# A residual graph-network kernel on one core: first pair's hop 2 in whole float32, bias sum ahead of it, square weights by partition, nine warm-up products, and another order of the last roots and stores

## The reference

```
Xw = x @ Wv + bv;  sj = Xw @ aw[:d];  si = Xw @ aw[d:]
alpha = adj * exp(leaky_relu(sj + si + ab, 0.2))
T = alpha / (rowsum(alpha) + 1e-12)
H = sum over k=0..2 of (T^k x) @ Wk[k] + bk[k]
x = layernorm(x + relu(H))
x = layernorm(x + (adj @ x) @ w)
```

## Time and profile before

| | us |
|---|---|
| median of 3 runs | 272.7 (272.46 to 272.84) |
| profiled execution, whole time | 272.39 |
| its span, first to last instruction | 270.6 |
| PE busy in the span | 264.1 |
| DVE busy | 216.7 |
| ACT busy | 193.0 |
| POOL busy | 191.5 |

### The profile page before, as it was taken

The page is one execution under the profiler, slowest core; times in us unless marked ns, Lnnn a source line. Parts: engine busy times, 40 slices in busy tenths (PEclk is TensorE's granted clock), DMA queues, the critical chain, the costliest instruction groups (busy, mean ns, idle before and its releaser), DMA issues.

```text
span 270.6 us, 6025 instructions
## 1 busy us (share of the span) xinstructions
PE 264.1 (98%) x1890; PEld 246.1 (91%) x1890; DVE 216.7 (80%) x615; ACT 193.0 (71%) x439; POOL 191.5 (71%) x412
## 2 busy tenths in 40 slices
PE   8899999999999999999999999999999999999992
PEld 5899999999999999999999999999999999999991
DVE  0777798888889888888988888988888898788984
ACT  4887767777666777766777766677776667766874
POOL 4665567778877778887777887777788777657533
PEclk9999999999999999999999999999999999999999
DMA  7997486828955488446873484943884457932214
GB/s 242 274 185 94 85 48 218 131 72 147 168 137 159 81 133 117 155 143 156 140 117 80 154 155 137 152 153 51 131 160 100 118 116 75 125 99 78 80 41 155
DMA packets 28342, 34.91 MB, mean 129 GB/s; under 512 B 6803, under 2 KB 16150, under 8 KB 28310
## 3 DMA queue, kind: packets, MB, share of 16 engines
q1 hardware_dynamic: 27888, 34.12, 60.8%
q10 hardware_dynamic: 422, 0.40, 0.4%
HBM read 26.09 MB, written 8.42 MB: 128 GB/s over the span
## 4 chain that ended last, share of the span: by engine, by line
PE 95%; DMA 2%; DVE 1%; SPq 0%; ACT 0%; issue 0%
PE ps_v L1107 31%; PE ps_y L1107 17%; PE ps_out L1107 15%; PE ps_h L1107 11%; PE ps_agg L1271 10%; PE ps_v L1204 3%; PE ps_v L1208 3%; PE ps_v L1206 3%; DMA WY_sb<-Wk_dram 2%; PE ps_agg L1107 2%; DVE last_out_sb L884 0%; PE ps_v L1254 0%; PE ps_h L1245 0%; PE ps_y L1245 0%; PE ps_agg L1254 0%; DVE WY_lo L669 0%
## 5 line engine op out<-in xcount | busy, mean ns | idle before, releaser
L1107 PE MATMUL ps_v<-WX_hi,XT_hi 128*128 128x512 f32 (+1 forms) x132 | 49.0, 371 | 0.0
L1107 PE MATMUL ps_v<-WX_lo,XT_hi 128*128 128x512 f32 (+1 forms) x132 | 48.6, 368 | 0.0
L1107 PE MATMUL ps_v<-WX_hi,XT_lo 128*128 128x512 f32 (+1 forms) x132 | 48.6, 368 | 0.0
L1029 POOL TENSOR_TENSOR XT_lo<-xt,XT_hi 128x512 fp32r<-128x512 f32 x32 | 42.1, 1319 | 6.6 <-ACT XT_hi L426 6.6
L1039 POOL TENSOR_TENSOR alpha<-exps,adjs 128x256 f32<-128x256 f32 x31 | 23.1, 744 | 28.9 <-ACT exps L470 28.8
L1043 POOL TENSOR_TENSOR alpha_lo<-alpha,alpha_hi 128x256 fp32r<-128x256 f32 x31 | 22.8, 735 | 19.4 <-ACT alpha_hi L479 19.4
L1107 PE MATMUL ps_y<-WY_hi,XT_hi 128*128 128x258 f32 x116 | 35.2, 303 | 0.6 <-DVE WY_lo L673 0.6
L503 ACT ACTIVATE y<-res,offset,rstd 128x256 f32<-128x256 f32 x62 | 33.6, 591 | 2.2 <-POOL offset L1005 2.2
L1271 PEld LDWEIGHTS ps_agg<-adjs,y 128*128 128x128 f32 x248 | 32.0, 191 | 2.2
L1271 PE MATMUL ps_agg<-adjs,y 128*128 128x128 f32 x248 | 32.7, 275 | 0.0
L1107 PE MATMUL ps_y<-WY_lo,XT_hi 128*128 128x258 f32 x116 | 32.7, 282 | 0.0
(11 more groups left out here) (179 smaller groups left out, 830.8 us busy)
## 6 DMA issues: line engine op xcount, KB each, us to landing
xt<-xt_dram SPq DMA_DIRECT2D x32, 256.0 KB, 5.7
nodes<-nodes_dram SPq DMA_DIRECT2D x32, 256.0 KB, 5.8
out_dram<-out_sb SPq DMA_DIRECT2D x30, 256.0 KB, 5.3
adjs<-adjs_dram SPq DMA_DIRECT2D x32, 128.0 KB, 5.7
spread<-si_rows_dram SPq DMA_DIRECT2D x29, 128.0 KB, 4.7
si_rows_dram<-scores SPq DMA_DIRECT2D x29, 1.0 KB, 3.9
WvT_sb<-WvT_dram SPq DMA_DIRECT2D x1, 260.0 KB, 3.6
W_sb<-Wk_dram ACTq DMA_DIRECT2D x1, 256.0 KB, 3.3
```

The source lines that it names most:

```text
L1029: pool.tensor_tensor(XT_lo[k % 7][:].rearrange("p c b i -> p (c b i)"), xt_sb[k % 4][:], XT_hi[k % 7][:].rearrange("p c b i -> p (c b i)") ...
L1107: last = pe.matmul(to, a, b, start=start and n == 0, stop=stop and n == 2, skip_group_check=True)
```

## The change

WY_sb gets two more columns, into which DVE copies the score weights, so that pair 0's hop 2 multiplies whole float32 operands (`first_hop2`) and needs neither WY_hi nor WY_lo. WY_lo is then made in one subtraction, behind W1's low part. Pair 1's hop 2 (`second_hop2`) does its six hi-by-x products first and those with XT_lo after them. `sum_of_biases` stands ahead of `score_shift` and writes to ps_v; bk_hi_of is ACT's first step, and bias_of_hops one of DVE's first. Half of hop2_and_scores(2) goes ahead of propagate_v2(0). load_xt(4) waits for y_done. W0, W1, W2 and w are laid out by partition on the host, 2 KB in one piece each (W2 with two zero columns in each chunk). keep_warm runs nine products. In the tail ACT takes root 0 between the two halves of pair 29's normalisation, DVE splits `last_normalise2` into inverse and output with the inverse of graph 0 ahead of the moments of graph 1, and SP stores graph 0 of pair 31 before the half of pair 30.

```diff
--- before.py
+++ after.py
@@ -16,11 +16,11 @@
 
-def resnorm_graph_kernel(nc, xt, adjs, nodes, WvT, Wk, bk, w, si_rows, out):
+def resnorm_graph_kernel(nc, xt, adjs, nodes, WvT, W0, W1, W2, bk, w, si_rows, out):
     PAIRS = nodes.shape[0]
-    D = w.shape[0]
+    D = bk.shape[1]
     C = D // P
-    HOPS = Wk.shape[0]
+    HOPS = bk.shape[0]
@@ -42,7 +42,7 @@
         W1_sb = sb("W1_sb", [P, C, D])
-        WY_sb = sb("WY_sb", [P, C, D])
+        WY_sb = sb("WY_sb", [P, C, D + 2])
@@ -122,7 +122,7 @@
         ps_shift = ps_agg[:, 1, 0:1]
-        ps_bias = ps_y[:, 0, 0:D]
+        ps_bias = ps_v[:, 1, 0:D]
@@ -309,6 +309,7 @@
 
+        first_X = xt_sb[0][:].rearrange("p (c b i) -> p c b i", c=C, b=PER)
@@ -319,7 +320,7 @@
 
-                    sp.wait_ge(h_done, 1)
+                    sp.wait_ge(y_done, 1)
@@ -359,8 +360,8 @@
             def load_Wk(n):
-                to = (W0_sb, W1_sb, WY_sb)[n]
-                sp.dma_start(to[:], Wk[n].rearrange("(c p) n -> p c n", p=P)).then_inc(Wk_loaded[n], DMA)
+                to, held = ((W1_sb, W1), (WY_sb, W2))[n - 1]
+                sp.dma_start(to[:].rearrange("p c n -> p (c n)"), held).then_inc(Wk_loaded[n], DMA)
@@ -397,18 +398,21 @@
                     load_adjs(4)
-                    sp.dma_start(w_sb[:], w.rearrange("(c p) n -> p c n", p=P)).then_inc(w_loaded, DMA)
+                    sp.dma_start(w_sb[:].rearrange("p c n -> p (c n)"), w).then_inc(w_loaded, DMA)
...
 
+            def store_last(b):
+                sp.wait_ge(last_out_ready, b + 1)
+                sp.dma_start(out[LAST, :, b * D:(b + 1) * D], last_out_sb[:, b]).then_inc(last_stored, DMA)
+
+            store_last(0)
...
             sp.dma_start(out[LAST - 1, :, 0:D], out_sb[(LAST - 1) % 3][:, 0]).then_inc(last_stored, DMA)
-            for b in range(PER):
-                sp.wait_ge(last_out_ready, b + 1)
-                sp.dma_start(out[LAST, :, b * D:(b + 1) * D], last_out_sb[:, b]).then_inc(last_stored, DMA)
+            store_last(1)
@@ -416,7 +420,7 @@
         def _(act):
-            act.dma_start(W0_sb[:], Wk[0].rearrange("(c p) n -> p c n", p=P)).then_inc(Wk_loaded[0], DMA)
+            act.dma_start(W0_sb[:].rearrange("p c n -> p (c n)"), W0).then_inc(Wk_loaded[0], DMA)
@@ -436,7 +440,7 @@
                 act.wait_ge(Wk_loaded[2], DMA)
-                act.activation(WY_hi[:, :, 0:D], WY_sb[:], ACT.Copy).then_inc(WY_hi_ready, 1)
+                act.activation(WY_hi[:, :, 0:D], WY_sb[:, :, 0:D], ACT.Copy).then_inc(WY_hi_ready, 1)
@@ -508,13 +512,14 @@
 
-            def late_normalise2(k):
+            def late_normalise2(k, graphs=range(PER)):
...
                 act.wait_ge(stored[k % 3], loads(k - 3, 3))
-                for b in range(PER):
+                for b in graphs:
...
                                           ACT.Identity, bias=offset2[k % 3][:, b:b + 1], scale=rstd2[k % 3][:, b:b + 1])
-                last.then_inc(late_out_ready, 1)
+                if b == PER - 1:
+                    last.then_inc(late_out_ready, 1)
@@ -614,11 +619,11 @@
 
+            bk_hi_of()
...
             wx_hi(1)
-            bk_hi_of()
@@ -653,8 +658,9 @@
             late_normalise2(LAST - 3)
-            late_normalise2(LAST - 2)
+            late_normalise2(LAST - 2, [0])
             last_std2_of(0)
+            late_normalise2(LAST - 2, [1])
@@ -665,15 +671,21 @@
 
-            dve.wait_ge(WY_hi_ready, 1)
-            dve.tensor_tensor(WY_lo[:, :, 0:D], WY_sb[:], WY_hi[:, :, 0:D].bitcast(F32), ALU.subtract)
-            dve.wait_ge(u_done, 1)
-            dve.tensor_copy(WY_hi[:, :, D:D + 2], ps_u).then_inc(u_ready, 1)
-            dve.wait_ge(u_ready, 1)
-            dve.tensor_tensor(WY_lo[:, :, D:D + 2], ps_u, WY_hi[:, :, D:D + 2].bitcast(F32),
-                              ALU.subtract).then_inc(WY_ready, 1)
-            dve.wait_ge(WX_hi_ready[1], 1)
-            dve.tensor_tensor(WX_lo[:, :, 0], W1_sb[:], WX_hi[:, :, 0].bitcast(F32), ALU.subtract).then_inc(WX_ready[1], 1)
+            def score_columns():
+                dve.wait_ge(Wk_loaded[2], DMA)
+                dve.wait_ge(u_done, 1)
+                dve.tensor_copy(WY_sb[:, :, D:D + 2], ps_u).then_inc(u_ready, 1)
+                dve.tensor_copy(WY_hi[:, :, D:D + 2], ps_u).then_inc(u_ready, 1)
+
+            def wy_lo():
+                dve.wait_ge(WY_hi_ready, 1)
+                dve.wait_ge(u_ready, 2)
+                dve.tensor_tensor(WY_lo[:], WY_sb[:], WY_hi[:].bitcast(F32), ALU.subtract).then_inc(WY_ready, 1)
+
+            def first_hop1_low():
+                dve.wait_ge(WX_hi_ready[1], 1)
+                dve.tensor_tensor(WX_lo[:, :, 0], W1_sb[:], WX_hi[:, :, 0].bitcast(F32),
+                                  ALU.subtract).then_inc(WX_ready[1], 1)
@@ -877,9 +889,11 @@
 
-            def last_normalise2(b):
+            def last_rstd2_of(b):
...
                 dve.reciprocal(last_rstd2[:, b:b + 1], last_std2[:, b:b + 1]).then_inc(last_rstd2_ready, 1)
+
+            def last_normalise2(b):
@@ -943,14 +957,17 @@
             bk_lo_of()
+            score_columns()
+            bias_of_hops()
             shift_of_scores()
+            first_hop1_low()
+            wy_lo()
...
             first_alpha_lo()
-            bias_of_hops()
@@ -979,9 +996,11 @@
             last_statistics2(1)
+            last_rstd2_of(0)
             last_mom2(1)
-            for b in range(PER):
-                last_normalise2(b)
+            last_normalise2(0)
+            last_rstd2_of(1)
+            last_normalise2(1)
@@ -1108,16 +1127,35 @@
 
+            def first_hop2():
+
+                pe.wait_ge(Wk_loaded[2], DMA)
+                pe.wait_ge(u_ready, 1)
+                for b in range(PER):
+                    for c in range(C):
+                        last = pe.matmul(hop2(0)[:, b, 0:D + 2], first_X[:, c, b], WY_sb[:, c], start=c == 0,
+                                         stop=c == C - 1, skip_group_check=True)
+                last.then_inc(y_done, 1)
+
+            def second_hop2():
+
+                pe.wait_ge(WY_ready, 1)
+                pe.wait_ge(shift_ready, 1)
+                pe.wait_ge(xt_hi_ready, 2)
+                for b in range(PER):
+                    for c in range(C):
+                        for n, W in enumerate((WY_hi, WY_lo)):
+                            pe.matmul(hop2(1)[:, b, 0:D + 2], XT_hi[1][:, c, b], W[:, c], start=c == 0 and n == 0,
+                                      stop=False, skip_group_check=True)
+                pe.wait_ge(xt_lo_ready, 2)
+                for b in range(PER):
+                    for c in range(C):
+                        last = pe.matmul(hop2(1)[:, b, 0:D + 2], XT_lo[1][:, c, b], WY_hi[:, c], start=False,
+                                         stop=c == C - 1, skip_group_check=True)
+                last.then_inc(y_done, 1)
+
             def hop2_and_scores(k, graphs=range(PER)):
-
-                if k == 0:
-                    pe.wait_ge(WY_ready, 1)
                 pe.wait_ge(xt_lo_ready, k + 1)
-
-                if k == 1:
-                    pe.wait_ge(shift_ready, 1)
-                if k == 2:
-                    pe.wait_ge(bias_ready, 1)
@@ -1131,9 +1169,8 @@
                 pe.wait_ge(Wk_loaded[0], DMA)
-                X = xt_sb[0][:].rearrange("p (c b i) -> p c b i", c=C, b=PER)
                 for c in range(C):
-                    last = pe.matmul(ps_h[:, b], X[:, c, b], W0_sb[:, c], start=b == 0 and c == 0, stop=c == C - 1,
+                    last = pe.matmul(ps_h[:, b], first_X[:, c, b], W0_sb[:, c], start=b == 0 and c == 0, stop=c == C - 1,
@@ -1141,6 +1178,8 @@
                 pe.wait_ge(WX_ready[1], 1)
+                pe.wait_ge(xt_lo_ready, 1)
+                pe.wait_ge(bias_ready, 1)
@@ -1309,7 +1348,6 @@
                 pe.wait_ge(bk_ready, 1)
-                pe.wait_ge(v2_lo_ready, 1)
@@ -1346,22 +1384,23 @@
 
-            keep_warm(ps_v[:, 0], 8)
+            keep_warm(ps_v[:, 0], 9)
...
             first_hop0(1)
+            sum_of_biases()
             score_shift()
-            hop2_and_scores(0)
+            first_hop2()
...
             first_hop1(1)
-            hop2_and_scores(1)
-            sum_of_biases()
+            second_hop2()
+            hop2_and_scores(2, [0])
...
             spread_scores(1)
-            hop2_and_scores(2)
+            hop2_and_scores(2, [1])
@@ -1402,9 +1441,15 @@
         np.concatenate([WvT, np.concatenate(columns).transpose(2, 1, 0)], axis=2).reshape(P, -1))
-    for name in ("Wk", "bk"):
-        arrays[name] = np.ascontiguousarray(inputs["L0_gnn_" + name])
-    arrays["w"] = np.ascontiguousarray(inputs["L1_gnn_w"])
+
+    def by_partition(m, room=0):
+        chunks = np.asarray(m).reshape(d // P, P, d).transpose(1, 0, 2)
+        return np.ascontiguousarray(np.pad(chunks, ((0, 0), (0, 0), (0, room))).reshape(P, -1))
+
+    for hop in range(3):
+        arrays[f"W{hop}"] = by_partition(inputs["L0_gnn_Wk"][hop], 2 if hop == 2 else 0)
```

(2 more changed lines are left out.)

## The result

The changed kernel took 273.37 us (median of 6 runs, 273.18 to 273.58) against 272.54 for the kernel before beside it (6 runs): ratio 1.0039, 95% interval 1.0030 to 1.0049. The profiled execution took 273.58, the longest of the six, with a span of 271.7; before it was 272.39 and 270.6. So 1.2 us came in where 0.3 were to go.

What follows compares the result with a forecast made beforehand. PE, 95% of the chain that ended last, was taken to bound the kernel, with pair 0's softmax chain setting propagate_v2(0). Head +0.03 and tail -0.30 summed to -0.27 us, from 272.7 to 272.4; range 271.8 to 273.0.

Steps and rivals of the forecast that it cites:

- What DVE and ACT do meanwhile costs nothing: Head, during pair 0's hop 2: DVE's and ACT's steps stay hidden, W1 low ready near 9.2, hop 1 wanting it at 9.62.
- a rival about ACT: Head, slower case: ACT's new first step and a slow XT_lo(0) delay the score shift; 273.1 to 273.3 us, chance 0.10.
- Bias sum moved ahead: Head, PE ahead of the score shift: two products on 3 rows cost +0.43 us, ends 0.24 and 0.55.
- The ninth product: Head, PE before hop 0: costs 0.43 us but takes over 0.29 of low clock; +0.14 us, ends 0 and +0.43.
- Hop 2 of pair 0 in whole float32: Head, PE: eight records of 1.74 us replace twelve split products of 1.54, +0.20 us, without needing WY_hi or WY_lo.
- The step on ACT: Head: bk_hi first puts XT_hi(0) at 4.6 and the shift's input at 7.28; PE wants it at 7.66, hidden by 0.4 us.
- SP's queue: Loads behind load_xt(4), which waits until about 9.9, are issued later but stay hidden, by 0.2 us at the least.
- Tail: After PE's last product: reordered roots, inverse and stores bring SP's last issue earlier; -0.30 us, ends -0.05 and -0.40.
- The two new halts of PE: Head: PE waits for V_lo before propagate_v1(0) and alpha_lo before propagate_v2(1), each under 0.4 us.
- The chain model: Head: pair 0's softmax chain has no slack, +0.15 us at propagate_v2(0); propagate_v2(1) at 18.14 against 18.11, +0.03.
- PE's order decides: Head rival: the two chains are shorter than they look, propagate_v2(1) starts at 17.51, kernel 271.8 us; chance 0.20.
- Nothing lands earlier at the end: Tail rival: data of the four last stores set the end, tail gives at most 0.05, kernel 272.7 us; chance 0.20.

Runs made afterwards that it cites:

- run 15: Run 5 with POOL's XT_lo(1) held back and nine products: 271.87 us against 272.33 for the kernel before, ratio 0.9989.
- run 4: Changed kernel with POOL's XT_lo(1) held back until W1's low part and WY_lo are made: 272.60 us against 272.32 for the kernel before, 1.0010.
- run 5: Changed kernel with bias sum, its parts and copy, and all of hop2(2) back in their old places: 273.71 us against 272.36 before, 1.0048, in three groups.
- run 10: Run 1 with bias sum and copy moved ahead of the shift and bk_hi first on ACT: 272.80 us against 272.30 for the kernel before, 1.0021.
- run 1: Kernel before with only the new tail (order of last roots and stores): 271.85 us against 272.32, ratio 0.9985.
- run 9: Changed kernel again with no edit, on another chip: 273.05 us against 272.30 for the kernel before, ratio 1.0020.
- run 11: Run 7 with ACT's XT_hi(2) moved behind pair 0's exponentials: 272.50 us against 272.30 for the kernel before, ratio 1.0011.
- run 3: Changed kernel with DVE's low part of W0 moved behind pair 0's alpha_lo: 273.10 us against 272.32 for the kernel before, ratio 1.0021.
- run 6: Changed kernel with pair 0's hop 2 split again, behind a WY_lo made before DVE's bias copy: 272.76 us against 272.36 for the kernel before, 1.0013.
- run 7: Run 5 with eight products and POOL's XT_lo(1) held back until DVE's two low parts are made: 271.78 us against 272.36 before, 0.9983.
- run 8: Kernel before with only W0 to W2 and w laid out in 2 KB pieces: 272.25 us against 272.36, ratio 0.9996.

## Why the prediction was wrong

Two steps failed, both in the head. Taking both away, as run 15 does, leads from 0.83 us above the kernel before to 0.46 below it, by medians; the first alone leads to 0.28 above (run 4).

**"What DVE and ACT do meanwhile costs nothing" failed.** It costed DVE's steps by their durations alone, 0.68 and 0.69, and gave W1's low part 0.4 us of cover. It was ready at 10.22 and not near 9.2, only 0.05 us ahead of hop 1's start, and behind it the backlog of 0.77 reached the softmax chain. Run 4 takes only this away and is 0.55 us (medians) to 0.8 us (ratios) faster than the changed kernel's first measurement, 0.47 and 0.3 than its second. The sign stood in the prediction's own text: two XT_lo from 8.48 in 3.45 us. It read this as POOL being slow and put it into a rival about ACT. POOL and DVE before:

```profile
8.48 2.19 POOL L1029 TENSOR_TENSOR XT_lo<-xt,XT_hi 128x512 fp32r<-128x512 f32 x1 [2.44 <-ACT XT_hi L426]
...
8.39 0.41 DVE L685 TENSOR_TENSOR bk_lo<-bk_sb,bk_hi 3x256 fp32r<-3x256 f32 x1
8.85 0.67 DVE L680 TENSOR_TENSOR WX_lo<-W_sb,WX_hi 128x512 fp32r<-128x512 f32 x1
```

It was POOL waiting for DVE's bk_lo and WX_lo: WX_lo ended at 9.52, XT_lo 1.15 later. The change turned the order round, and DVE waited for POOL.

**"Bias sum moved ahead" was undersized, and the idleness did not absorb it.** Forecast +0.43, by rows 0.53 up to the shift (6.83 + 0.94 = 7.77 would be its start without the bias, and it is 8.30) and 0.62 up to hop 2 (run 5 against 4). The 0.09 between the two is the delay on the way back to products of 128 rows, which the forecast had only in its upper end, 0.55. Why each delay is some 0.1 is not shown; in its new place the bias also stands between whole float32 products. The old place, just ahead of a halt for alpha_lo, was nearly free; the new one is on the path. Runs 15 and 4 differ by the bias's place, with its parts and its copy, and hop2(2)'s: 0.9989 against 1.0010, 0.6 us, by medians 0.74 (on two chips, and the intervals just overlap). Run 10, which moves it alone, lost 1.0 us against run 1. By the rule of the Trainium skill ("TensorE: Matmul & The Clock Gate", "Step-by-step: what each phase is for"), by which a weight load's row count does not matter, the prediction had 0.24. The loads themselves agree with the page, 0.18 us for 3 rows and 0.19 for 128 in the changed kernel; the starts of the products do not follow from it.

**"The ninth product": +0.14 held over the profiles together, and not in a single execution.** In run 4 the score weights start at 5.44, 0.10 later than before; in the changed kernel's profile at 6.02. The first four hop 0 records took 0.86 to 1.47 behind nine products and 0.94 to 1.84 behind eight. Over all profiles the score weights start at 5.11 to 6.02 behind nine (nine profiles, middle 5.44) and at 5.01 to 6.29 behind eight (eight profiles, middle 5.27): 0.17 between the middles. The clock rises at another moment in each execution, and the forecast took one execution's 0.29 of low clock for a constant. Nor was "data did not make PE wait" constant: W0 came 0.16 late in run 9 and 0.42 late in run 11. What this adds to the loss over the runs is not settled; between the changed kernel's two profiles it was 0.5 us.

**"Hop 2 of pair 0 in whole float32" missed a part.** Its own length was right: 1.64 in runs 4 and 5 against 1.74. But the second product of hop 1 starts 0.31 behind the first there instead of 0.12. From hop 2's start to the spread of the scores that makes 2.54 in run 4 against 2.25 before: +0.29, and not +0.20.

**Right.** All 0.56 of idleness gone. The step on ACT: bk_hi at 4.08, XT_hi(0) at 4.40, the shift's input at 7.07 against 7.28 forecast. So the slower rival's mechanism, the shift late behind XT_lo(0), didn't happen; that its time, 273.1 to 273.3, came close to the measured 273.37 is chance. SP's queue: load_xt(4) was issued at 10.56, and no wait of ACT or PE for x followed. Tail: -0.31 against -0.30. The two new halts of PE came, for V_lo ahead of propagate_v1(0) (18.61) and for alpha_lo ahead of propagate_v2(1) (19.49), and propagate_v2(0) followed alpha_lo's end by 0.25 as it had by 0.26. The chain model lets 0.12 of the delay vanish between propagate_v2(0) and (1); measured were 1.63 and 1.38, and 1.44 at PE's last load. So the model held and what went into it did not: the delay at hop 1 was 0.80 instead of 0.15, and at propagate_v2(0) 1.63 instead of 0.15.

"PE's order decides" did not come about: in the changed kernel alpha_lo was later still, and even in run 4 propagate_v2(1) started at 18.19, not near 17.5. "Nothing lands earlier at the end" falls by run 1's rows.

**Open.** The cause of run 5's groups, 1.5 us apart, and the share of the clock in the loss over the runs. No whole float32 hop 2, ninth product or layout was shown to gain: run 15 has all three, and run 1 none, and they take 271.87 and 271.85.

## What to carry to other kernels

Before a step on one engine is costed by its duration, look whether the same operation has two durations in the trace, and what the neighbour does meanwhile: a transfer of waiting from POOL to DVE can cost where the work itself is unchanged. An idle gap ahead of a chain can be a reserve against what varies between executions; work moved into it is paid in the executions that needed it. Work that stands beside a halt can be free where it stands, as the bias sum nearly was, and is paid in full ahead of the chain that ends in the halt. And where a kernel's executions differ by more than the change is worth, one profile gives the mechanism and not the price.

## What the runs showed of the hardware

DVE's and POOL's subtractions with both inputs in SBUF don't run at once. Alone they take 0.68 and 1.27 us for 128x512; when held up, each ends 0.54 to 0.55 (DVE) or 1.13 to 1.16 (POOL) after the other's end, in the changed kernel and in runs 3, 6 and 9. DVE's with one input in PSUM (V_lo, 0.68 at 10.72 in the kernel before, beside POOL's XT_lo of 1.30) is not held up. The Trainium skill says this in "SBUF — State Buffer", under "Who interferes with whom": a DVE instruction with two SBUF inputs contends with a GpSimd instruction that reads SBUF, and the issue order decides who blocks. The trace agrees on who contends, with these numbers. On the order it agrees in the changed kernel and in runs 3, 6 and 9, but not everywhere: in the kernel before and in runs 7, 11 and 15 an XT_lo that began beside bk_lo was still held while W0's low part, which began 0.37 us (0.11 in the runs) after it, ran in its usual 0.67, and XT_lo ended 1.15 to 1.17 behind that.

The level of PE's clock after the first products: the first four hop 0 records took 0.89 us in run 4 and 1.84 in runs 8 and 10, which is 2.4 and 1.2 GHz.
